# Mixture of experts in sorted blocks of 128 rows, with indirect DMA, in a one-core decoder layer

## The chip, the core and the metric

The kernel runs on one core of a Trainium2 chip. The metric is the device time of one execution in microseconds (us); less is better. Five engines work side by side and meet at semaphores: PE (TensorE, matrix products; its weight loads are listed apart, as PEld), DVE (VectorE), ACT (ScalarE), POOL (GpSimd) and SP (SyncE, which here only issues DMAs). A name with a q (SPq, POOLq) is the sequencer of that engine. A DMA issued by SP or POOL runs on 16 DMA engines that all queues share.

## What is computed

x has 8 batches of 112 tokens of 512 numbers. Three residual steps follow each other: causal self attention, cross attention to a context, and a feed-forward step with experts. Only the last step changes in its algorithm:

```
def _moe(x, gate, expert_bias, w1, w2, w3, shared_w1, shared_w2, shared_w3):
    scores = sigmoid(xt @ gate.T)                        # 896 tokens, 8 experts
    _, sel = top_k(scores + expert_bias, 2)
    top_scores = take_along_axis(scores, sel, axis=1)
    routed = xt[token_idx] * scores_sorted[:, None]      # 1792 rows, one for each choice
    xb = routed.astype(bfloat16)
    for e in range(8):
        h = silu(xb @ w1[e].T) * (xb @ w3[e].T)          # 512 -> 256, bfloat16
        oe = h @ w2[e].T                                 # 256 -> 512
        out_r = out_r + where(expert_ids == e, oe, 0.0)
    hs = silu(xt @ shared_w1.T) * (xt @ shared_w3.T)
    out = hs @ shared_w2.T                               # shared expert, float32
    return out.at[token_idx].add(out_r)
```

The tokens are layer-normalised first, and x is added at the end. Every token has two experts of eight; which ones they are is known only when the gate's scores are there.

## The kernel before

`attention` does both attention steps. Its second part, cross attention, runs 16 steps n (four turns u of four batches s), from about 215 us to 518 us. In each step POOL normalises seven tiles of probabilities (`x_normalise`, L1421) and makes the low parts of the weights that were loaded for the next turn (L1427, L1432). SP loads these weights and contexts in turn order, and waits between them for PE.

`experts` does the last step, in 128-partition tiles of turned tokens (channels on the partitions, tokens in the free dimension), in two halves h of 448 tokens:

- SP loads gate, bias and small tables, writes x to HBM (`x_dram`, L1554) and reads it back in tiles of 128 tokens (`x7`, L1557). POOL loads the experts' matrices with a cast from float32 to bfloat16: w13 of each expert into two buffers (L1569, L1575), w2 of all at once (L1570).
- DVE normalises (`fxn`, L1727). PE turns the eight batches (L1583, into `r_ps`), ACT copies them (`xt`, L1684), DVE makes the high and low parts (L1732, L1716), and PE multiplies all eight batches by the gate (L1590).
- PE runs the shared expert's up projection in four units (`shared_unit`, two for each half; each 24 products of 448 columns, lines 55 to 57). DVE meanwhile takes sigmoid, the two best experts and the weights (L1741 to L1754).
- PE turns the weights (L1650) and spreads an expert's weights over 128 partitions (`spread`, L1610, L1636). DVE scales all tokens by them (`scale_input`, L1771).
- `expert`: for each of 8 experts and both halves, PE does 2 x 16 products of 448 columns (L1624) with a tile of the expert's matrix held in the array and the tokens streamed past it. All 896 tokens go through all 8 experts; a token's weight is zero where it did not choose the expert. ACT takes silu (L1692), DVE multiplies (`hidden`, L1778).
- For seven tiles of 128 tokens, PE adds up 16 products of 512 columns for the experts (L1671) and six of the shared expert in one PSUM bank; DVE adds x (L1807), SP stores (L1561).

PE's program is in order. In `mm3` a float32 product is made of three products of high and low parts:

```
    pe.matmul(out, a_hl[0], b_hl[0], start=start, stop=False, skip_group_check=True)
    pe.matmul(out, a_hl[0], b_hl[1], start=False, stop=False, skip_group_check=True)
    return pe.matmul(out, a_hl[1], b_hl[0], start=False, stop=stop, skip_group_check=True)
```

Of the kernel before, what the change touches and what calls it, by code (L numbers as in the profile page):

```python
# [23 lines left out]
KC = C // 128  # L24
# [13 lines left out]
HC = HID // 128  # L38
EPS = 1e-5
# [48 lines left out]
def build(nc, a, out):  # L88
    with ExitStack() as keep:
# [25 lines left out]

        dve_chain = sem("dve_chain")
        chain_end = [0]

        with ExitStack() as ctx:
            attention(nc, a, sem, sb, ctx, ident, x_sb, xn2_hl, w_raw, p_raw, mask, stats_all, ow_dram, kvn_dram, kvt_dram, aw_dram,  # L120
                      sw_raw, sw_hl, sd_raw, sd_hl, dve_chain, chain_end)
        sb("shared_room", [128, 6 * KC * HID])
        experts(nc, a, sem, sb, ident, x_sb, xn2_hl, sw_hl, sd_hl, stats_all, dve_chain, chain_end, out)


def attention(nc, a, sem, sb, ctx, ident, x_sb, xn2_hl, w_raw, p_raw, mask, stats_all, ow_dram, kvn_dram, kvt_dram, aw_dram,
              sw_raw, sw_hl, sd_raw, sd_hl, dve_chain, chain_end):
# [70 lines left out]
    tile("tail_rest", [128, 936])  # L198
# [59 lines left out]
    qw_loaded, qw_high, qw_low = ([sem(f"qw_{w}{i}") for i in range(4)] for w in ("loaded", "high", "low"))  # L258
    ow_loaded, ow_high, ow_low = ([sem(f"ow_{w}{i}") for i in range(4)] for w in ("loaded", "high", "low"))
# [5 lines left out]
    out_done, x_added = sem("xout_done"), sem("x_added")  # L265
    sw_loaded, sd_loaded, sh_high, sh_low = sem("sw_loaded"), sem("sd_loaded"), sem("sh_high"), sem("sh_low")
# [9 lines left out]
    def ring(n):  # L276
        return FIRST if n == 0 else STARTS if n % HALF == 0 and n < STEPS else LATER

# [25 lines left out]
    with nc.Block() as block:  # L304
        @block.sync
        def _(sp):
# [87 lines left out]
            for u in range(TURNS):  # L394
# [30 lines left out]
        def _(pe):  # L425
# [145 lines left out]
            def query_pair(n, i):  # L571
# [3 lines left out]
                pe.wait_ge(qw_low[i], u + 1)  # L575
# [61 lines left out]
            def x_project(m, i):  # L637
# [4 lines left out]
                pe.wait_ge(ow_low[i], m // HALF + 1)  # L642
# [151 lines left out]
        def _(act):  # L794
# [96 lines left out]
            def x_query_weights_high(u, i):  # L891
                if u < TURNS:
                    act.wait_ge(qw_loaded[i], 32 * u + 32)
                    act.copy(qw[:, i, 0, :], qw_raw[:, i, 1, :]).then_inc(qw_high[i], 1)

            def out_weights_high(u, i):
                act.wait_ge(ow_loaded[i], 16 * u + 16)
                act.copy(ow[i][:, 0], ow_raw[i][:, 1]).then_inc(ow_high[i], 1)  # L898
# [481 lines left out]
        def _(pool):  # L1380
# [43 lines left out]
            def query_weights_low(u, i):  # L1424
                if u < TURNS:
                    pool.wait_ge(qw_high[i], u + 1)
                    pool.tensor_tensor(qw[:, i, 1, :], qw_raw[:, i, 1, :], qw[:, i, 0, :],  # L1427
                                       ALU.subtract).then_inc(qw_low[i], 1)

            def out_weights_low(u, i):  # L1430
                pool.wait_ge(ow_high[i], u + 1)
                pool.tensor_tensor(ow[i][:, 1], ow_raw[i][:, 1], ow[i][:, 0], ALU.subtract).then_inc(ow_low[i], 1)  # L1432

            def shared_low(part):
                pool.wait_ge(sh_high, part + 1)
                raw, high, low = SHARED[part]
                pool.tensor_tensor(low, raw, high, ALU.subtract).then_inc(sh_low, 1)

# [48 lines left out]
def experts(nc, a, sem, sb, ident, x_sb, xn_hl, sw_hl, sd_hl, stats_all, dve_chain, chain_end, out):  # L1487


    HALVES = 2  # L1490
    TILES = N // 128
    x_dram = nc.dram_tensor("x_dram", (N, C), F32).ap()
    rows = out.rearrange("b t c -> (b t) c")
    with ExitStack() as ctx:
# [5 lines left out]
        x7 = tile("x7", [128, TILES, C])  # L1500
        tile("fxn_rest", [128, B * C - TILES * C])
        mean, rstd = tile("mean3", [T, B, 2]), tile("rstd3", [T, B])
        vv, newt = tile("vv3", [T, B]), tile("newt3", [T, B])
        xt = tile("xt", [128, KC, N])
        xt_hl = xn_hl
        gate = tile("gate", [128, KC, EXPERTS])
        bias = tile("bias", [T, EXPERTS])
        iota = tile("iota", [T, EXPERTS])
        pick = tile("pick", [EXPERTS, EXPERTS, 128])
        pick_r = tile("pick_r", [EXPERTS, EXPERTS, 128], F32R)  # L1510
        score = tile("score", [T, B, EXPERTS])
        ranked = tile("ranked", [T, B, EXPERTS])
        best = tile("best", [T, B, 8])
        which = tile("which", [T, B, 8], U32)
        whichf = tile("whichf", [T, B, 2])
        chosen = tile("chosen", [T, 2, B, EXPERTS])
# [360 lines left out]
```

## Time and profile before

| | us |
|---|---|
| median of 3 runs | 661.54 (661.42 to 664.84) |
| the profiled execution | 666.14 |
| its span, from first to last instruction | 664.5 |
| experts stage in it, from 519.3 to 664.5 | 145.2 |

| engine | busy, us | share of the span |
|---|---|---|
| PE | 603.0 | 91% |
| PEld | 460.5 | 69% |
| DVE | 397.4 | 60% |
| ACT | 287.4 | 43% |
| POOL | 246.8 | 37% |

The profile is of one execution. Times of rows are microseconds from the start of the span. The end of a matrix product is modelled, so products that overlap in the pipeline have durations (0.36 us) that are longer than their distance (0.20 us); the chain of work shows the distances. PEclk is the clock granted to PE as a share of full speed.

### The profile page before, as it was taken

Reading aid. Unit: us, or ns where it says so; the run is one execution under the profiler, and the core shown is the slowest. Engines: PE = TensorE matmul, PEld = TensorE weight load, DVE = VectorE, ACT = ScalarE, POOL = GpSimd, SP = SyncE. Lnnn points to the kernel's source line nnn. Section 1 sums busy time; section 2 is a strip of 40 time slices with the busy share of each in tenths; the row PEclk is TensorE's granted clock in tenths of the full one; section 3 lists DMA queues with packets and bytes.
Section 4 is the critical chain, followed back from the end, with each engine's and each line's share of the span. In section 5 each row is a group of like instructions: output and inputs, shape, how many; then the busy total and the mean of one; then the engine's idle time right before and its main releaser. Section 6 shows DMA issues by size and latency. Waiting matters only on the chain. (4 is left out here: it accounts for less than half of the span.)

```text
span 664.5 us, 9657 instructions
## 1 busy us (share of the span) xinstructions
PE 603.0 (91%) x3583; PEld 460.5 (69%) x3586; DVE 397.4 (60%) x844; ACT 287.4 (43%) x629; POOL 246.8 (37%) x225
## 2 busy tenths in 40 slices
PE   2668898998989699999999999999998699999798
PEld 1445676665767488879888888879887498444354
DVE  6654677686675676457664666457663754788411
ACT  3123441633635476447763576447753212322100
POOL 0508732643833355406851387406842100000000
PEclk9968897998979899999999999999999669999899
DMA  8843555665533050013111330005000671343011
GB/s 271 230 151 100 189 178 172 220 193 181 209 127 108 6 152 0 1 50 135 68 47 56 135 111 0 1 14 194 16 1 0 133 227 57 51 76 63 1 48 63
DMA packets 24817, 67.09 MB, mean 101 GB/s; under 512 B 3035, under 2 KB 6573, under 8 KB 24389
## 3 DMA queue, kind: packets, MB, share of 16 engines
q1 hardware_dynamic: 23476, 60.20, 27.4%
q0 software_dynamic: 1296, 6.29, 5.1%
q8 instruction: 29, 0.48, 0.3%
q14 instruction: 16, 0.12, 0.1%
HBM read 56.66 MB, written 16.11 MB: 110 GB/s over the span
## 5 line engine op out<-in xcount | busy, mean ns | idle before, releaser
L1421 POOL TENSOR_TENSOR xprob<-xprob,erec 128x375 f32<-128x375 f32 x112 | 90.2, 812 | 142.6 <-DVE erec L1200 142.4
L888 ACT ACTIVATE xprob<-s_ps,nmax 128x375 f32<-128x375 f32 x112 | 64.2, 574 | 59.8 <-DVE nmax L1195 56.9
L1195 DVE TENSOR_REDUCE nmax<-s_ps 128x1 f32<-128x375 f32 x112 | 59.6, 538 | 0.0
L55 PE MATMUL k_ps<-ow,ctx_hl 128*112 128x512 f32 x128 | 52.5, 410 | 2.8 <-DVE ctx_hl L1190 2.1
L1624 PE MATMUL gu_ps<-xb,w 128*128 128x448 bf16 x256 | 51.2, 353 | 0.4 <-DVE h_all L1778 0.4
L57 PE MATMUL k_ps<-ow,ctx_hl 128*112 128x512 f32 x128 | 50.5, 395 | 0.0
L1190 DVE TENSOR_TENSOR ctx_hl<-k_ps,ctx_hl 128x448 fp32r<-128x448 f32 x32 | 20.0, 624 | 50.6 <-ACT ctx_hl L883 50.6
L56 PE MATMUL k_ps<-ow,ctx_hl 128*112 128x512 f32 x128 | 50.2, 392 | 0.0
L1170 DVE TENSOR_TENSOR pt_hl<-f_ps,pt_hl 125x512 fp32r<-125x512 f32 (+1 forms) x67 | 41.7, 623 | 11.1 <-ACT pt_hl L860 9.8
L55 PE MATMUL s_ps<-kvt,qt_hl 128*128 128x376 f32 x112 | 44.9, 401 | 2.0 <-ACT xprob L888 1.0
L1414 POOL TENSOR_TENSOR prob<-prob,rec 112x1792 f32<-112x1792 f32 x8 | 25.5, 3186 | 54.8 <-DVE rec L1136 54.8
L1692 ACT ACTIVATE act_sb<-gu_ps 128x448 f32<-128x448 f32 x36 | 19.6, 543 | 59.1 <-PE gu_ps L1624 39.8
L860 ACT CAST pt_hl<-f_ps 125x512 fp32r<-125x512 f32 (+1 forms) x67 | 35.6, 533 | 14.1 <-PE f_ps L618 13.8
L1624 PEld LDWEIGHTS gu_ps<-xb,w 128*128 128x128 bf16 x256 | 23.7, 98 | 25.9 <-issue 4.7
L1432 POOL TENSOR_TENSOR ow<-ow_raw,ow 128x1024 fp32r<-128x1024 f32 x16 | 38.3, 2392 | 7.7 <-ACT ow L898 7.7
L618 PEld LDWEIGHTS f_ps<-ident,xprob 128*125 128x125 f32 x236 | 35.4, 189 | 3.8 <-DVE pt_hl L1170 1.0
L56 PE MATMUL s_ps<-kvt,qt_hl 128*128 128x376 f32 x112 | 37.6, 336 | 0.0
L618 PE MATMUL f_ps<-ident,xprob 128*125 128x128 f32 x236 | 37.5, 277 | 0.1
L57 PE MATMUL s_ps<-kvt,qt_hl 128*128 128x376 f32 x112 | 37.6, 335 | 0.0
L55 PE MATMUL k_ps<-pt_hl,kvn 125*128 125x448 f32 x96 | 35.4, 369 | 0.0
L57 PE MATMUL k_ps<-pt_hl,kvn 125*128 125x448 f32 x96 | 35.1, 366 | 0.0
L56 PE MATMUL k_ps<-pt_hl,kvn 125*128 125x448 f32 x96 | 34.9, 364 | 0.0
(208 smaller groups left out, 1495.9 us busy)
## 6 DMA issues: line engine op xcount, KB each, us to landing
ow_raw<-ow_dram SPq DMA_DIRECT2D x16, 512.0 KB, 3.3
raw_b<-in_raw SPq DMA_DIRECT2D x8, 640.0 KB, 5.0
raw_m<-in_raw SPq DMA_DIRECT2D x8, 576.0 KB, 4.8
raw_q<-in_raw SPq DMA_DIRECT2D x8, 512.0 KB, 6.6
ow_dram<-bw_sb SPq DMA_DIRECT2D x8, 512.0 KB, 5.9
qw_raw<-aw_dram SPq DMA_DIRECT2D x16, 256.0 KB, 3.5
w<-in_w POOLq DMA_DIRECT2D x8, 512.0 KB, 5.1
kvt_dram<-kvt_hl SPq DMA_DIRECT2D x8, 376.0 KB
```

Of the source, the lines that this page charges most:

```text
L55: pe.matmul(out, a_hl[0], b_hl[0], start=start, stop=False, skip_group_check=True)
L56: pe.matmul(out, a_hl[0], b_hl[1], start=False, stop=False, skip_group_check=True)
L57: return pe.matmul(out, a_hl[1], b_hl[0], start=False, stop=stop, skip_group_check=True)
L618: mm = pe.transpose(bank[0:LP, j * 128:(j + 1) * 128], xprob[slot(n - 1, k)][:, c * LP:(c + 1) * LP], ident[:, :])
L860: act.copy(dst, src).then_inc(high_copied, 1)
L888: act.activation(xprob[z][:, 0:L], s_bank(n, k)[:, 0:L], ACT.Exp, bias=nmax[:, z:z + 1], accum_out=esum[:, z:z + 1]).then_inc(xexp_done, 1)
L1170: dve.tensor_tensor(dst, src, hi, ALU.subtract).then_inc(emptied, 1)
L1195: dve.tensor_reduce(nmax[:, z:z + 1], s_bank(n, k)[:, 0:L], X, ALU.max, negate=True).then_inc(xmax_done, 1)
L1414: pool.tensor_tensor(prob[q][:, :, :, :], prob[q][:, :, :, :], rec[q][:, :, :].unsqueeze(3).broadcast_to([T, PER, GROUPS, T]), ALU.mult).t ...
L1421: pool.tensor_tensor(xprob[z][:, 0:L], xprob[z][:, 0:L], erec[:, z:z + 1].broadcast_to([128, L]), ALU.mult).then_inc(xp_ready, 1)
L1432: pool.tensor_tensor(ow[i][:, 1], ow_raw[i][:, 1], ow[i][:, 0], ALU.subtract).then_inc(ow_low[i], 1)
L1624: mm = pe.matmul(gu_ps[m][:, w, 0:HT], w13[z][:, w, k, m * 128:(m + 1) * 128], xb[h][:, k, :], start=(k == 0), stop=(k == KC - 1))
```

## The change

In the experts stage the two choices of a token become rows of a table that is sorted by expert, and each expert works only on its own rows, in blocks of 128.

- In cross attention, POOL clears a small tile and numbers the table's spare rows (`lay_blank`, at step 1), and SP fills two tables in HBM (`slots_dram`, one for each half, 14 blocks of 128 rows of 544 bfloat16 each) with zeros and row numbers, behind the loads of turn 0. POOL issues ten DMAs from HBM to HBM, one at the end of each of the steps 2 to 11, that cast w13 and w2 to bfloat16. The semaphores of the weight halves become four common ones instead of 16.
- SP loads all of w13 and w2 (6 MB of bfloat16) at the start of the experts stage. x is not written to HBM and read back any more.
- Turning and gate are done by halves. ACT makes the high part of the turned tokens too.
- `choose`, `count`, `locate`, `owners`: the two best experts of each token; PE counts with a triangular matrix how many tokens before it chose the same expert; DVE works out the row of each choice in the sorted table and the expert that owns each block.
- `lay_rows`: DVE scales the normalised tokens by their weight, in bfloat16, once for each choice. POOL scatters them with 16 indirect DMAs of 112 rows. The order of DVE's program is by halves; `count(1)` of PE stands between the shared units 1 and 2 and waits for `choose(1)`.
- The shared expert's down projection gets a stage of its own: eight batches, x is added in place.
- 28 blocks g. SP loads the block's 128 rows into one of six slots (`xg`); PE turns them (four transposes), ACT copies; PE holds the turned rows and streams the owner's w1 and w3 past them (`up`, four products of 512 columns, the expert's number read into a register by `value_load`); silu on ACT, product on DVE; PE turns the result (two transposes), ACT copies, PE multiplies by w2 (`down`, two products of 512 columns); DVE copies to one of four tiles `o_sb`; POOL scatters the 128 rows with an indirect DMA to HBM (`done_dram`). The list of indices lies in the block's slot.
- SP loads for each token its two rows back (`got`), PE adds them with an identity matrix in one PSUM bank, DVE adds x, SP stores.

The core of the diff:

```diff
+                if u == 0:
+                    sp.wait_ge(blank_ready, 2)
+                    for h in range(HALVES):
+                        rows = slots_dram[h].rearrange("(j p) c -> p j c", p=128)
+                        sp.dma_start(rows[:, :, 0:C], blank[:, :].bitcast(BF16).unsqueeze(1).broadcast_to([128, BLOCKS, C])).then_inc(rows_laid, 16)
+                        sp.dma_start(rows[:, :, C:ROW].bitcast(I32), spare[:, :, :]).then_inc(rows_laid, 16)
...
+                if n == 1:
+                    lay_blank()
+                if 2 <= n < 2 + EXPERTS:
+                    pool.dma_start(w13_dram[n - 2], a["w13"][n - 2]).then_inc(w_cast, 16)
+                if 2 + EXPERTS <= n < 4 + EXPERTS:
+                    z = n - 2 - EXPERTS
+                    es = slice(z * EXPERTS // 2, (z + 1) * EXPERTS // 2)
+                    pool.dma_start(w2_dram[:, es], a["w2"][:, es]).then_inc(w_cast, 16)
...
+    RING, SENT = 6, 4
+    EARLY = BLOCKS + RING + 1
...
+                def load_slots(g):
+                    h, j, z = g // BLOCKS, g % BLOCKS, g % RING
+                    if j == 0:
+                        sp.wait_ge(sent[h], 16 * TOP2 * HALF)
+                    if g >= RING:
+                        sp.wait_ge(xg_turned, g - RING + 1)
+                        sp.wait_ge(put[(g - RING) % SENT], 16 * put_by(g - RING + 1)[(g - RING) % SENT])
+                    sp.dma_start(xg[z][:, :], slots_dram[h][j * 128:(j + 1) * 128]).then_inc(xg_loaded[z], 16)
...
+                for g in range(ALL):
+                    pool.wait_ge(o_copied, g + 1)
+                    to = xg[g % RING][:, C:C + 2].bitcast(U32)
+                    pool.indirect_dma_start(done_dram[g // BLOCKS], bass.IndirectOffsetOnAxis(ap=to, axis=0),
+                                            o_sb[g % SENT][:, :], None).then_inc(put[g % SENT], 16)
...
+                def up(g):
...
+                    e = pe.value_load(own_e[0:1, h, j:j + 1], min_val=0, max_val=EXPERTS - 1)
+                    pe.wait_ge(xg_copied, g + 1)
+                    wait(pe, hid_done, g - 1)
+                    for k in range(KC):
+                        mm = pe.matmul(b_ps[g % 2][:, :], xgt[g % 2][:, k, :], w13[:, e, :, k, :], start=(k == 0), stop=(k == KC - 1))
...
+                shared_unit(0)
+                count(0)
                 shared_unit(1)
...
+                count(1)
                 shared_unit(2)
...
                 shared_unit(3)
...
+                for b in range(B):
+                    shared_down(b)
+                pe.wait_ge(tri_ready, 3)
+                pe.wait_ge(d_added, B)
+                turn_slots(0)
+                turn_slots(1)
+                pe.wait_ge(w_loaded, 16 * 6)
+                owner = [up(0)]
+                for g in range(ALL):
+                    if g + 2 < ALL:
+                        turn_slots(g + 2)
+                    if g + 1 < ALL:
+                        owner.append(up(g + 1))
+                    turn_hidden(g)
+                    if g:
+                        down(g - 1, owner[g - 1])
+                    if EARLY <= g < EARLY + HALF:
+                        gather(g - EARLY)
+                down(ALL - 1, owner[ALL - 1])
+                for b in range(HALF, B):
+                    gather(b)
...
+                shared_hidden(0)
+                locate(0)
+                for b in range(HALF):
+                    lay_rows(b)
+                choose(1)
+                owners(0)
+                shared_hidden(1)
+                shared_hidden_low(0)
+                locate(1)
...
+                for g in range(ALL):
+                    hidden(g)
+                    if g >= 2:
+                        copy_out(g - 2)
+                    if EARLY < g <= EARLY + HALF:
+                        result(g - EARLY - 1)
```

## Rows read from the trace of the kernel before

**Rows 1.** Busy time by stretch: us (instructions) per engine, PEclk, DMA share, GB/s
```profile
246.00:290.00 44.00, 44.00 (x244) 38.43 (x243) 24.97 (x57) 24.19 (x59) 19.23 (x19) 1.00 0.00 1
...
320.00:420.00 100.00, 99.97 (x555) 87.83 (x554) 62.29 (x149) 62.13 (x151) 55.67 (x54) 1.00 0.19 66
...
519.00:540.00 21.00, 15.94 (x98) 14.79 (x99) 14.55 (x49) 4.52 (x10) 1.78 (x3) 0.60 0.88 191
...
565.00:625.00 60.00, 56.41 (x273) 26.61 (x271) 47.69 (x50) 17.56 (x33) 3.16 (x6) 1.00 0.31 53
625.00:664.50 39.50, 35.62 (x151) 18.75 (x154) 4.96 (x8) 0.00 (x0) 0.00 (x0) 0.94 0.13 47
```

**Rows 2.** Chain that ended last, experts stage: start, us on it, engine, tile, line, count
```profile
524.06 6.47 PE r_ps L1583 x32
530.53 9.06 PE w_ps L1590 x64
539.59 0.57 PE gu_ps L55
...
551.26 0.77 PE w_ps L1650 x8
...
556.85 1.00 PE r_ps L1610 x4
...
566.65 3.19 PE gu_ps L1624 x16
...
625.51 5.09 PE gu_ps L1671 x15
...
651.48 3.47 PE gu_ps L1671 x16
656.35 3.47 PE gu_ps L1671 x16
```

**Rows 3.** Instructions grouped by line, from 508 to 665 us: busy us, mean ns
```profile
L1692 ACT ACTIVATE act_sb<-gu_ps 128x448 f32<-128x448 f32 x36 | 19.6, 543 | 59.1 <-PE gu_ps L1624 39.8 <-PE gu_ps L57 19.3
...
L1807 DVE TENSOR_TENSOR y_sb<-x,gu_ps 128x512 f32<-128x512 f32 x7 | 4.8, 687 | 32.1 <-PE gu_ps L57 32.1
L1684 ACT COPY xt<-r_ps 128x448 f32<-128x448 f32 x8 | 4.2, 533 | 13.0 <-PE r_ps L1583 13.0
L1727 DVE TENSOR_SCALAR fxn<-x_sb,mean,rstd 112x512 f32<-112x512 f32 x8 | 3.7, 538 | 0.0
```

**Rows 4.** Timeline: start, us, engine, line; transposes, and DVE from scores to weights
```profile
500.16 1.04 PE L618 MATMUL f_ps<-ident,xprob 128*125 128x128 f32 x8
...
539.88 0.20 DVE L1741 TENSOR_SCALAR score<-score 112x64 f32<-112x64 f32 x1 [5.39 <-ACT score L1686]
...
545.77 0.23 DVE L1754 TENSOR_TENSOR chosen<-chosen,score 112x64 f32<-112x64 f32 x1
...
547.07 0.63 DVE L1759 TENSOR_TENSOR hs<-gu_ps,act_sb 128x448 f32<-128x448 f32 x1 [1.07 <-ACT act_sb L1692]
```

**Rows 5.** Busy time by stretch, around PE's idle time ahead of L1671
```profile
622.00:625.50 3.50, 0.00 (x0) 0.13 (x2) 2.76 (x5) 0.36 (x1) 0.00 (x0) 1.00 0.00 0
625.50:629.10 3.60, 3.59 (x9) 1.31 (x9) 0.00 (x0) 0.00 (x0) 0.00 (x0) 0.53 0.02 5
```

**Rows 6.** DMA issues: count, KB each, median us to landing; last, POOL's issuing instruction in ns
```profile
w<-in_w POOLq DMA_DIRECT2D x8, 512.0 KB, 5.1
...
out<-y_sb SPq DMA_DIRECT2D x7, 256.0 KB, 2.0
...
qw_raw<-in_kr SPq DMA_DIRECT2D x16, 64.0 KB, 3.3
...
L1575 POOL DMA_DIRECT2D w<-in_w x6: 527/527/527, 570.5 to 607.8; - x6
```

**Rows 7.** Timeline of POOL in cross attention, end of one step and start of the next
```profile
260.14 1.55 POOL L1427 TENSOR_TENSOR qw<-qw_raw,qw 128x640 fp32r<-128x640 f32 x1
263.60 0.81 POOL L1421 TENSOR_TENSOR xprob<-xprob,erec 128x375 f32<-128x375 f32 x1 [1.91 <-DVE erec L1200]
```

More of the change, by code:

```diff
@@ L38 @@
 HC = HID // 128
+HALVES, TOP2 = 2, 2
+BLOCKS = TOP2 * HT // 128 + EXPERTS - 1
+ROW = C + 32
+SPARE = TOP2 * HT
 EPS = 1e-5
@@ L1509, in experts @@
[L1509 to L1516, printed above, removed]
-        wt_hl = tile("wt_hl", [EXPERTS, 2, N], F32R)
-        w13 = [tile(f"w13_{z}", [128, 2, KC, HID], BF16) for z in range(2)]
+        with ExitStack() as laid:
+            xt = sb("xt", [128, KC, N], F32, laid)
@@ L1547, in experts, with put_by @@
+        def put_by(g):
+            return [sum(1 for k in range(g) if k % SENT == z) for z in range(SENT)]
         with nc.Block() as block:
@@ new lines, in turn_hidden, with down @@
+                def turn_hidden(g):
+                    pe.wait_ge(hid_done, g + 1)
+                    wait(pe, hid_copied, g)
+                    bank = h_ps[:, :].bitcast(BF16)
+                    for m in range(HC):
+                        mm = pe.transpose(bank[:, m * 128:(m + 1) * 128], hid[g % 2][:, m * 128:(m + 1) * 128], ident_bf[:, :])
+                    mm.then_inc(hid_turned, 1)
+                def down(g, e):
+                    pe.wait_ge(hid_copied, g + 1)
+                    wait(pe, o_copied, g - 1)
+                    for m in range(HC):
+                        mm = pe.matmul(o_ps[g % 2][:, :], hid_t[g % 2][:, m, :], w2[:, e, m, :], start=(m == 0), stop=(m == HC - 1))
+                    mm.then_inc(o_done, 1)
@@ new lines, in gather @@
+                def gather(b):
+                    pe.wait_ge(got_loaded[b // HALF], 16 * HALF)
+                    wait(pe, y_ready, b)
+                    for r in range(TOP2):
+                        mm = pe.matmul(c_ps[0:T, :], ident_bf[0:T, 0:T], got[:, b, r, :], start=(r == 0), stop=(r == TOP2 - 1))
+                    mm.then_inc(c_done, 1)
+                for b in range(HALF):
+                    turn_tokens(b)
+                pe.wait_ge(small_loaded, 64)
+                route(0)
@@ new lines, in _ @@
+                for b in range(B):
+                    shared_down(b)
[15 more added lines that the diff above has]
+                        gather(g - EARLY)
@@ new lines, in lay_rows, with shared_hidden @@
+                def lay_rows(b):
+                    h, s = b // HALF, b % HALF
+                    for r in range(TOP2):
+                        dve.tensor_scalar(rows[:, b, r, 0:C], xn[:, b, :], weight[:, h, r, s:s + 1], None,
+                                          ALU.mult).then_inc(rows_ready, 1)
+                def shared_hidden(u):
+                    half, m = u // HC, u % HC
+                    dve.wait_ge(silu_done, u + 1)
+                    dve.tensor_tensor(hs[:, m, half * HT:(half + 1) * HT], gu_ps[u % 2][1][:, 0:HT], act_sb[u % 2][:, :],
+                                      ALU.mult).then_inc(h_done, 1)
@@ new lines, in hidden, with copy_out @@
+                def hidden(g):
+                    dve.wait_ge(up_silu, g + 1)
+                    wait(dve, hid_turned, g - 1)
+                    dve.tensor_tensor(hid[g % 2][:, :], b_ps[g % 2][:, HID:2 * HID], up_sb[g % 2][:, :], ALU.mult).then_inc(hid_done, 1)
+                def copy_out(g):
+                    z = g % SENT
+                    dve.wait_ge(o_done, g + 1)
+                    if g >= SENT:
+                        dve.wait_ge(put[z], 16 * put_by(g)[z])
+                    dve.tensor_copy(o_sb[z][:, :], o_ps[g % 2][:, :]).then_inc(o_copied, 1)
@@ new lines, in _ @@
+                for b in range(HALF):
+                    tile_low(b)
+                choose(0)
+                for b in range(HALF, B):
+                    tile_low(b)
+                shared_hidden(0)
+                locate(0)
+                for b in range(HALF):
+                    lay_rows(b)
[4 more added lines that the diff above has]
+                locate(1)
+                for b in range(HALF, B):
+                    lay_rows(b)
@@ L1811 @@
+                copy_out(ALL - 1)
+                for b in range(HALF, B):
+                    result(b)
 def kernel(**inputs):
```

532 lines of the change are left out of this document (304 added, 228 removed).

## The prediction

> **What bounds the kernel now.** I read the busy time by stretch first. Through cross attention PE has work for 99.97 of 100 us at full clock, while POOL has 56 [rows 1]: PE is the bound there, and what the change adds on POOL and SP costs only what reaches PE. In the experts stage PE is busy 56.4 of the 60 us of the experts' up projection and 35.6 of the last 39.5 us, with the DMA engines at 31% and 13% [rows 1]. The chain of work that ended last says the same: it runs over PE's products one behind the other [rows 2]. So the stage of 145.2 us (519.3 to 664.5) is bound by PE's columns, and fewer columns would help. The first 21 us are another matter: clock 0.60, DMA engines at 88% [rows 1]. DMA latency is nowhere on the chain; every transfer of this stage is loaded early or stored late. The question for the change is whether it stays so.
>
> **Part 1, cross attention.** POOL gets ten DMA issues. One took 0.53 us, for 128 rows [rows 6]; they stand where POOL sat idle for 1.91 us between two steps [rows 7], so I cost them at nothing. Without that cover it would be 10 x 0.53 = 5 us. POOL's two small instructions at step 1 go with them. The transfers themselves use engines that are 19% busy [rows 1]. SP's four fills (3.7 MB) wait for POOL's step 1 and start near 254 us. Behind them on SP stand only the loads of turn 1, from 289 us, and the DMA engines moved nothing from 246 to 290 us [rows 1], so 35 us of cover. The removed semaphores only merge counts that rise in the same order. I take 0 for the whole part, and -1 to +5 as bounds.
>
> **Part 2, up to the shared expert.** Turning takes 6.47 us for 8 batches and the gate 9.06 us [rows 2]; by halves they are the same instructions on PE in another order. ACT now copies each batch twice, 2 x 0.53 us [rows 3], against 0.81 us of turning, but the gate products between the halves let it catch up. So the first shared unit begins at 539.6, as before [rows 2]. The write of x to HBM goes away; nothing waited for it. From 539.59 to 551.26 there are two units, and one unit at full clock takes 556.85 - 552.03 = 4.82 us [rows 2]; the first, half of it at the lower clock, takes 6.85. The counting is some eight small products like L1650, 0.8 us [rows 2]. PE: unit 0 to 546.5, count(0) to 547.3, unit 1 to 552.1.
>
> Now count(1) waits for choose(1), and DVE is late. Its program: shared_hidden(0) ends at about 547.9 (before it was 547.07 + 0.63 [rows 4]); locate(0) has 9 small instructions of 0.2 us (as L1741 [rows 4]), 1.9 us; eight lay_rows at 3.7 us for eight (L1727 [rows 3]); choose(1): scores to weights took 539.88 to 546.00 for eight batches [rows 4], for four some 4.0. That is 557.5, so PE idles 5.4 us, with units 2 and 3 queued behind the wait. What this does to the clock is in the trace: PE was idle for 3.5 us (622.0 to 625.5) and then ran 3.6 us at 0.53 [rows 5], its 15 products taking 5.09 us where 16 take 3.47 later [rows 2]. That is 1.8 us more; I take 2.0. So count(1) to 558.4, unit 2 to 565.2, unit 3 to 570.0. The shared down projection: two tiles of the last stage are 656.35 - 651.48 = 4.87 us apart, less the experts' 3.47 [rows 2] is 1.40 us for six products; times 8 batches is 11.2, to 581.2. It was inside the last stage before, 7 x 1.40 = 9.8. The loop then waits for the last addition (0.69, L1807 [rows 3], and 0.2): 582.1. The rows of both halves are scattered and loaded by then (DVE's last rows are laid near 567, eight indirect DMAs behind). 6 MB of weights go at the 191 GB/s of the first stretch [rows 1] in 33 us, to about 555: covered.
>
> **Part 3, PE's work in a block.** Four products of 512 columns for up and two for down, at 3.47/16 = 0.217 us [rows 2]: 1.30 us. Six transposes of 128 rows: eight took 1.04 us with the pipeline's end, some 0.12 apart [rows 4], and I take 0.1: 0.6. Together 1.9; with bubbles 2.0 us. 28 blocks are 56 us, against the 60 + 7 x 3.47 = 84 us for the experts before. ACT has three instructions a block, 0.58 + 0.37 + 0.37 scaled from 0.53 and 0.54 us for 448 columns [rows 3], 1.3 us; DVE 0.4 + 0.6 = 1.0. Neither binds. value_load stands ahead of each up; the trace has nothing like it. Bounds: 0 (PE's queue covers it) and a round trip as long as the shortest DMA, 2.0 [rows 6]; I take 0, since the sequencer reaches it with the last down and the next transposes, 0.8 us, still to run, and since the next part leaves room for it. The Trainium skill (DMA: Bandwidth & Descriptors, Latency and other measured facts) gives such a load a floor of 0.6 us; by that it would be covered too. No row here shows it.
>
> **Part 4, the slots' ring.** This is what I expect to decide. Slot g is loaded only when block g-6's scatter has landed, because its index list lies in that slot. down(g-6) is the last work of PE's round g-5, and turn_slots(g) the first of round g-2: PE has two rounds between, 4 us. On the other side lies a chain of memory round trips:
> - down's end to o_sb copied: 0.2 pipeline end, 0.15 behind hidden(g-4), 0.6 for 512 columns (L1807 took 0.69 with two inputs [rows 3]): 0.95;
> - the indirect scatter of 128 KB, not in the trace. Lower bound 2.0, the store of 256 KB by SP; upper bound 5.1, POOL's casting load of 512 KB [rows 6]. It is a small store, near the lower row, plus POOL's work for 128 indices, for which I put twice POOL's 0.53 us issue [rows 6]: 3.1;
> - SP's load of 136 KB: between 2.0 and 3.3 [rows 6], taken as 2.2;
> - semaphores: 0.2.
>
> Sum 6.45 us for two rounds, so 3.2 us a block and not 2.0. With the bounds: 5.0 and, with 5.1 and 3.3, 9.6; I hold 8.2 for likely enough. The ring acts on rounds 4 to 25: 11 pairs. Up(0) ends at 582.1 + 0.4 + 0.7 + 0.9 = 584.1; three rounds to 590.1; 11 x 6.45 = 71.0, to 661.1; three more rounds to 666.6. The four-deep ring of o_sb asks 0.6 + 3.1 + 0.1 every four blocks and is slack.
>
> The page named above (Anatomy of one DMA — SWDGE (gpsimd) path) puts a DMA of POOL at about 2.0 us plus its bytes, 2.3 us for the scatter. By that the ring turns in 5.65 and the sum below ends near 671. It would give 4.4 us for the 1 MB source of w, and the row has 5.1 [rows 6].
>
> **Part 5, the tail.** After the last round: down 0.65, copy 0.65, scatter 3.1, three more issues of SP of 0.45 each, load 2.2, then a chain in one PSUM bank: 4 x (two products 0.65 + addition 0.69 + 0.05) = 5.5, store 2.0, end 0.5: 16.0. Before, only a store lay behind PE.
>
> **Sum.** 666.6 + 16.0 = 682.6 against a span of 664.5: +18.1. The profiled execution took 666.14 and the runs' median is 661.54, so the span is 3 us over the median; I add the difference to the median: 679.6.
>
> **Rivals.**
> - *The ring is slack* (faster than before). If scatter and load together take under 4.0 - 1.15 = 2.85 us, PE's 2.0 us is the pace: 584.1 + 56 + 16 = 656.1, -8.4, so 653.1. For it: the DMA engines are idle. Against it: already two of the shortest transfers of the trace are 4.0 [rows 6].
> - *PE falls to the lower clock in the loop.* At 1.2 GHz a block is 1.85 x 2 = 3.7 us: 584.1 + 103.6 + 16 = 703.7, so 700.8. For it: the ring gives PE gaps of 2.5 us every two rounds, and 3.5 us of idling lowered the clock [rows 5]. Against it: the gaps are shorter, and at 3.7 us a block there is no gap left. A slow value_load of 2 us gives the same number. The Trainium skill (TensorE: Matmul & The Clock Gate, HAM oscillation) tells of kernels in which each round starts cold behind a DMA wait; by it this rival holds, and the trace agrees as far as its one long gap goes.
> - *Cross attention suffers*: casts or fills delay PE. With part 1's upper bound 684.6, and more where casts are slow.
> - *The blocks save no columns.* Not so: 28 x 128 rows are padded, but their count is fixed, 3584 rows for 7168.
>
> **How the numbers follow.** Forecast (ring binds) 0.62, with its own range 662 (5.0 us, shorter tail) to 701 (8.2 us); ring slack 0.12; lower clock or slow register load 0.18; cross attention 0.08. A measurement of this kernel can tell some 0.5% (3.3 us) from no change. Faster: the slack ring and 0.04 of the forecast's low end, 0.16. Same: 0.08 from the low end, where the round trips are near 5.0, and 0.01 of the rest, 0.09. Slower 0.75. The range goes from 655, just above the slack ring, to 704, just above the lower clock.
>
> **What would show it.** In the profile after: idle time of PE ahead of the slots' transposes, released by the DMA of xg, in every second round, and turn_slots 6.4 us apart for two rounds; POOL's indirect DMAs with some 3 us to landing; a gap of 5 us ahead of count(1), with a lower clock behind it; the last down some 16 us ahead of the end; PE still 99.97 of 100 us busy in cross attention. I am wrong if an indirect DMA and a load together land within 3 us, if PE's rounds are even, if value_load holds PE longer than the ring does, or if the waits inside the loop end at POOL, because an indirect DMA keeps it for more than 3.2 us.

## The result, and the profile after

| | before | after |
|---|---|---|
| median, us | 663.19 (661.42 to 665.28, 4 runs) | 694.21 (692.97 to 699.51, 4 runs) |
| ratio, 95% interval | | 1.0482 [1.0413, 1.0551] |
| profiled execution, span | 666.14, 664.5 | 693.14, 691.3 |

The change makes the kernel 4.8% slower. Predicted were 679.6 us with a range of 655 to 704: the side is right, the size is 14.6 us short of the measured time. The span and the busy time of the page after:

```profile
span 691.3 us, 10138 instructions
PE 584.0 (84%) x3552; PEld 455.8 (66%) x3552; DVE 391.8 (57%) x908; ACT 307.0 (44%) x688; POOL 294.2 (43%) x290
```

Busy time by stretch: in cross attention, from the start of the experts stage to its first block, in the loop, behind it, and the whole stage (columns as in [rows 1]):

```profile
320.00:420.00 100.00, 99.97 (x545) 87.20 (x545) 61.29 (x148) 60.51 (x149) 57.40 (x59) 1.00 0.37 96
...
515.00:587.00 72.00, 55.78 (x256) 49.28 (x256) 38.48 (x144) 12.95 (x27) 18.61 (x34) 0.74 0.36 128
589.00:669.00 80.00, 56.60 (x330) 28.38 (x327) 29.26 (x57) 32.70 (x81) 23.73 (x25) 0.91 0.34 102
670.00:691.00 21.00, 5.16 (x12) 1.23 (x10) 4.07 (x6) 0.14 (x1) 2.92 (x3) 0.59 0.37 112
...
514.00:691.00 177.00, 119.11 (x608) 79.94 (x608) 73.64 (x209) 47.29 (x111) 45.87 (x62) 0.81 0.34 111
```

The same view of before, from 519 to 664 us:

```profile
519.00:664.00 145.00, 132.96 (x639) 81.57 (x642) 79.82 (x145) 27.79 (x52) 4.94 (x9) 0.91 0.34 82
```

The blocks do save PE work: 119.1 us of it in this stage where there were 133.0. But the stage is 177 us long and no longer 145: PE idles 58 us in it, where it idled 12. Those are the lines to explain. Who PE waited for, by stretch: first from the stage's start to the first block, then in the loop. Columns: us in total, times, longest.

```profile
PE e_ps L59 <- DVE x_sb L1960: 7.9, 1, 7.9
PE e_ps L1686 <- DVE fxn L1988: 6.3, 1, 6.3
PE e_ps L1705 <- DVE both L1910: 3.8, 1, 3.8
```

```profile
PE e_ps L1744 <- DMA xg<-slots_dram: 17.7, 9, 2.7
PE e_ps L1755 <- issue: 3.7, 9, 0.6
PE e_ps L1755 <- ACT xgt L1843: 1.9, 3, 0.7
```

The 6.3 us at L1686 are not new: before waits 6.2 us for the same products. New are the 7.9 us at L59 (called the hole below), the 3.8 us at L1705 and the waits of L1744 and L1755 in the loop. L1744 turns a slot, and it waits nine times for the load of xg. One turn of the ring, in the chain that ended last (start, us, what):

```profile
593.45 0.69 DVE o_sb L1972
594.15 0.27 issue
594.41 2.42 DMA done_dram<-o_sb,xg
...
596.89 2.47 DMA xg<-slots_dram
599.37 0.05 issue
599.41 0.41 PE e_ps L1744 x4
```

That is the chain that the prediction drew: copy, scatter 2.42, load 2.47, some 6.2 us from the end of down. Yet the timeline of PE shows the wait in every third round, not in every second:

```profile
599.41 0.40 PE L1744 MATMUL e_ps<-fident_bf,xg 128*128 128x128 bf16 x4 [2.66 <-DMA xg<-slots_dram]
...
601.93 0.39 PE L1744 MATMUL e_ps<-fident_bf,xg 128*128 128x128 bf16 x4
...
603.94 0.39 PE L1744 MATMUL e_ps<-fident_bf,xg 128*128 128x128 bf16 x4
604.54 1.03 PE L1755 MATMUL e_ps<-w,xgt 128*128 x4 [0.21 <-issue]
...
608.47 0.40 PE L1744 MATMUL e_ps<-fident_bf,xg 128*128 128x128 bf16 x4 [2.35 <-DMA xg<-slots_dram]
609.32 1.89 PE L1755 MATMUL e_ps<-w,xgt 128*128 x4 [0.46 <-issue]
```

Three rounds take 9.06 us here. The round behind a wait may run at the lower clock: the four products of L1755 took 1.89 us at 609.32 and 1.03 at 604.54.

### The profile page after: what moved, and what is told of

Read it like the earlier page. It is cut to its first block and busy times, and to the rows that moved or that the text cites. A ratio compares the mean times of both kernels' runs of the same rounds, so it can differ in the third digit from the quotient of the medians.

```text
span 691.3 us, 10138 instructions
## 1 busy us (share of the span) xinstructions
PE 584.0 (84%) x3552; PEld 455.8 (66%) x3552; DVE 391.8 (57%) x908; ACT 307.0 (44%) x688; POOL 294.2 (43%) x290
## 5 line engine op out<-in xcount | busy, mean ns | idle before, releaser
L1677 POOL DMA_INDIRECT done_dram<-o_sb,xg x28 | 27.2, 971 | 77.5 <-DVE o_sb L1972 76.9
L59 PE MATMUL k_ps<-ow,ctx_hl 128*112 128x512 f32 x128 | 52.5, 410 | 2.5 <-DVE ctx_hl L1215 1.9
L60 PE MATMUL k_ps<-ow,ctx_hl 128*112 128x512 f32 x128 | 50.2, 392 | 0.0
L1195 DVE TENSOR_TENSOR pt_hl<-f_ps,pt_hl 125x512 fp32r<-125x512 f32 (+1 forms) x67 | 41.7, 623 | 11.2 <-ACT pt_hl L885 10.1
L59 PE MATMUL s_ps<-kvt,qt_hl 128*128 128x376 f32 x112 | 45.1, 403 | 2.0 <-ACT xprob L913 1.0
L1965 DVE TENSOR_TENSOR hid<-e_ps,up_sb 128x256 bf16<-128x256 f32 x28 | 11.9, 425 | 51.4 <-ACT up_sb L1849 49.6
L60 PE MATMUL s_ps<-kvt,qt_hl 128*128 128x376 f32 x112 | 37.8, 337 | 0.0
L1755 PE MATMUL e_ps<-w,xgt 128*128 x112 | 32.5, 417 | 6.2 <-issue 3.7
L61 PE MATMUL s_ps<-kvt,qt_hl 128*128 128x376 f32 x112 | 37.7, 337 | 0.0
L59 PE MATMUL k_ps<-pt_hl,kvn 125*128 125x448 f32 x96 | 35.4, 368 | 0.0
```

Of the source, the lines that this page charges most:

```text
L1195: dve.tensor_tensor(dst, src, hi, ALU.subtract).then_inc(emptied, 1)
L1677: pool.indirect_dma_start(done_dram[g // BLOCKS], bass.IndirectOffsetOnAxis(ap=to, axis=0), o_sb[g % SENT][:, :], None).then_inc(put[g % S ...
L1755: mm = pe.matmul(b_ps[g % 2][:, :], xgt[g % 2][:, k, :], w13[:, e, :, k, :], start=(k == 0), stop=(k == KC - 1))
```

## The experiments

Each states its ratio to the kernel before, with 95% interval, where it was timed against it. S(i) is the start of the slots' transposes (L1744) in round i, which turn slot i+2. "First block" is the start of the very first of them, counted from the first statistics of the experts stage (514.96 us in the changed kernel, 519.83 in before).

### Ring of eight slots, and of five

```diff
-    RING, SENT = 6, 4
+    RING, SENT = 8, 4
-    EARLY = BLOCKS + RING + 1
+    EARLY = BLOCKS + 7
```

The other kernel has 5 in the place of 8. The kernel with eight slots also merges two semaphores with others, which the lines above leave out.

> Ring of gathered slots of 8 instead of 6 (two semaphores merged with others of the same engine to make room; nothing else is moved). In the trace of the changed kernel a round of the loop starts 6.4 us after the round that last used its slot has gone out: copy 0.7, scatter 2.4, load 2.4 and the issues. Its work lies in the round itself, so the recurrence there is over three rounds: 3 rounds in work 2.0-2.5 + 6.5 = 9.1-9.9 us. Theory A (slot ring): with 8 slots it is over five rounds, 8.5/5 = 1.7 us, below TensorE's own 1.9 us; the idle between rounds goes, rounds 3 to 25 take 22 x 1.9 = 42 us where they took 70.8, and the whole 664 to 670 us. Rival B (rate of the indirect DMAs or of the memory): the pace stays 3.0-3.2 us a block however many slots there are, 690-696 us. Rival C (clock): TensorE drops to the half clock at the loop's duty and a round costs 2.9 us, 685-694 us.

> Ring of 5 slots instead of 6, nothing else changed. Two readings of the ring give different doses. As the prediction put it (a slot's 6.45 us chain over R-4 rounds: two rounds with six slots): 6.45 us for every round, rounds 3 to 25 take 142 us, whole 765 us. As the trace of the changed kernel shows (work of one round 2.0-2.5 us plus 6.5 us over R-3 rounds): 4.3-4.5 us a round, 95-99 us, whole 718-723 us. If the ring does not set the pace: 694 us.

Eight slots: 665.21 us, ratio 1.0015 [0.9983, 1.0047]; S(3) to S(25) takes 48.9 us (588.61 to 637.48) instead of 70.8 (594.80 to 665.59). Five slots: 730.45 us, one run; S(3) to S(25) takes 106.6 us (594.52 to 701.10), 4.8 a round. Eight slots came out in the expected range. Five came out above the 718 to 723 us that were expected from the second reading, though far from the 765 of the first. PE's waits in the loop with five slots, and the timeline of PE with eight:

```profile
PE e_ps L1744 <- DMA xg<-slots_dram: 39.2, 12, 5.0
```

```profile
602.25 0.39 PE L1744 MATMUL e_ps<-fident_bf,xg 128*128 128x128 bf16 x4
602.69 1.03 PE L1755 MATMUL e_ps<-w,xgt 128*128 x4
603.57 0.28 PE L1764 MATMUL e_ps<-fident_bf,hid 128*128 128x128 bf16 x2
603.68 0.60 PE L1771 MATMUL e_ps<-w,hid_t 128*128 x2
604.11 0.39 PE L1744 MATMUL e_ps<-fident_bf,xg 128*128 128x128 bf16 x4
```

1.86 us a round, no wait. So the ring decides, and neither the rate of the DMAs (rival B) nor the clock (rival C) does: both fall, since the same transfers now go at 1.9 us a block. The dose settles how the ring counts. The chain, some 6.5 us with the signals, starts at the *end* of round i-3, and round i-3 has its own 2.0 to 2.5 us of work behind its start: from wait to wait S(i) = S(i-3) + 8.6 to 9.9 with six slots (up to S(19)), and mostly S(i) = S(i-2) + 9.4 with five. The prediction's own form (6.45 us for every round with five slots) asked for 142 us and 765. The second reading asked for 95 to 99 us where 106.6 were measured; it had taken 2.0 to 2.5 us for the work of a round, and with five slots both rounds of a turn ran at the lower clock (the four products of L1755 took 1.89 and 1.91 us at 614.23 and 617.40, against 1.03 above). The 48.9 us, against 42 expected, hold one thing more, ahead of slot 22 in round 20:

```profile
625.68 0.61 PE L1744 MATMUL e_ps<-fident_bf,xg 128*128 128x128 bf16 x4 [3.30 <-DMA xg<-slots_dram]
626.53 1.89 PE L1755 MATMUL e_ps<-w,xgt 128*128 x4 [0.25 <-issue]
```

SyncE had issued the four loads of got (L1636, 0.9 MB) at 617.91 to 619.91, and the load of this slot behind them at 620.02. So the wait is put down to them. In the kernel with four edits below, where these loads are spread over four slot loads, the wait at this place is gone.

### Rows of the second half scattered late

```diff
                 for g in range(ALL):
...
+                    if g < TOP2 * HALF:
+                        send_rows(1, g // TOP2, g % TOP2)
```

with the eight scatters of the second half taken out ahead of the loop.

> The eight scatters of the second half of the tokens are issued one behind each of the loop's first eight scatters and no longer while the shared part runs (which needs them only at round 14). Theory S (the storm of scattered rows holds up TensorE's signals): the hole of 7.9 us in the shared part ahead of the third sum, where ScalarE's activation of the last shared unit starts at 571.1 although its matmuls were streamed by 564.6, goes, and with it the half clock behind it (3 us); the loop begins 10 us earlier and the whole takes 684 us. Against it stands that GpSimd then spends 2.5 us a block in the first eight rounds (under the 3.2 of the ring; 0 to 4 us more). Rival T (the hole has nothing to do with the scatters, say a fetch of instructions at that place): hole stays at the same instruction, 694 to 698 us.

689.41 us, ratio 1.0403 [1.0358, 1.0448], where 684 was expected. The hole is not there and the first block starts 63.2 us behind the stage's start (72.5 in the changed kernel). This alone says nothing about the scatters, since the kernels with eight and with five slots, which ran on the same chip, keep the scatters and show no hole either; the run that can tell stands below. From the first block to the last product of a block it takes 85.4 us. The changed kernel takes 83.0, 85.0 and 85.1 in its three traces, so no loss in the loop is shown. POOL does hold two DMAs a block, 1.25 to 1.28 us each, and a ring scatter queues behind a row scatter:

```profile
588.67 0.94 POOL L1670 DMA_INDIRECT slots_dram<-rows,slot_u  x1 [0.30 <-issue]
589.92 0.97 POOL L1680 DMA_INDIRECT done_dram<-o_sb,xg  x1 [0.31 <-issue]
```

### VectorE chooses for the second half first

```diff
-                for b in range(HALF):
-                    lay_rows(b)
                 choose(1)
+                for b in range(HALF):
+                    lay_rows(b)
```

> VectorE picks the second half's experts before it writes the first half's 8 rows tiles (3.25 us) instead of behind them; nothing else changed. Theory: TensorE's idle of 3.75 us ahead of the second count falls to 0.5 or nothing, and the 3.4 us at half clock behind it goes (1.5 us): up to 4-5 us earlier, 689-690 us; the first half's scatters begin 3 us later, and that must not show, since the loop begins 30 us behind them. Rival: if the hole of 7.9 us further on is tied to the scatters (which now end no earlier), it grows by what is gained here: 694 us.

685.14 us, ratio 1.0311 [1.0248, 1.0375]. The wait ahead of the second count is down from 3.8 us to 0.5, as expected:

```profile
PE e_ps L59 <- DVE hs_hl L1956: 2.0, 1, 2.0
PE e_ps L1744 <- issue: 0.8, 1, 0.8
PE e_ps L1705 <- DVE both L1910: 0.5, 1, 0.5
```

Its first block starts at 61.5 us. Against the 65.1 of both ring kernels, which have the old order, that is 3.6 us for the order. The time is under the 689 to 690 us expected, because the hole is not in this trace either.

First blocks have to be compared with an eye on the clock. The late-rows kernel began its first block at 63.2 us here and at 65.3 in its second trace (below), with the same waits (3.7 and 1.4 us): the granted clock from the first shared unit to the first block was 0.92 and then 0.86. Over the four shared units it was 0.88 in the first trace of the changed kernel as in the first late-rows trace, and 0.78 in the kernel with eight slots as in the second late-rows trace. So of the 11 us between 61.5 and 72.5, 3.6 are the order and 9.4 (72.5 - 63.2) the hole with the lower clock behind it, less some 2 that the clock of the shared units gave back.

### The hole: the changed kernel again, and again

> The changed kernel itself, not a letter changed. In its first trace TensorE streamed the last shared unit's matmuls by 564.6 us, but the signal behind them is recorded at 571.08, together with those of the two sums behind it (571.15, 571.23), and in that hole of 7.9 us lies half of what the prediction missed ahead of the loop. None of the four kernels with one edit each shows the hole. Theory F (belongs to this program, whatever the cause): the same hole at the same signal, loop begins at 587 to 588, 693 to 695 us. Rival G (an event of one execution): no hole, the loop begins at 579 to 582, the profiled run takes 684 to 688, and the median of the runs lies between 684 and 694.

> The changed kernel once more, not a letter changed. Both traces of it show the hole: signals of TensorE that arrive 5 to 6.5 us behind the end of their matmuls, together, while the second half's rows are scattered and the first slots are loaded; with it the updates of VectorE and ScalarE of these 10 us are missing from the trace. The traces of the four kernels with one edit each show none, but they ran together on another chip than the second trace of the changed kernel, so program and chip can't be told apart yet. Theory F (the program's): hole again, first block of the loop at 72 us after the start of the experts' stage, 692 to 700 us. Rival K (the chip's, or the occasion's): no hole, first block at 65 us, 684 to 689 us.

696.18 and 696.81 us, first block at 72.1 and 72.2 us, and the hole in both. ScalarE's activations of the last two shared units (L1833), in the first trace of the changed kernel, in its second, and in the kernel with eight slots:

```profile
561.10 0.55 ACT L1833 ACTIVATE act_sb<-e_ps 128x448 f32<-128x448 f32 x1 [11.08 <-PE e_ps L61]
571.10 0.54 ACT L1833 ACTIVATE act_sb<-e_ps 128x448 f32<-128x448 f32 x1 [9.01 <-remote]
```

```profile
567.41 0.55 ACT L1833 ACTIVATE act_sb<-e_ps 128x448 f32<-128x448 f32 x1 [12.46 <-remote]
576.04 0.54 ACT L1833 ACTIVATE act_sb<-e_ps 128x448 f32<-128x448 f32 x1 [7.63 <-remote]
```

```profile
562.98 0.54 ACT L1833 ACTIVATE act_sb<-e_ps 128x448 f32<-128x448 f32 x1 [10.90 <-PE e_ps L61]
567.78 0.55 ACT L1833 ACTIVATE act_sb<-e_ps 128x448 f32<-128x448 f32 x1 [3.80 <-PE e_ps L61]
```

The two units are 4.8 us of PE apart, as in the last fence. They come 10.0 and 8.6 us apart where the hole is. "Remote" says that the signal came so long after the product that it can't be paired with it: PE streamed the unit's last product at 564.24 and its signal is recorded at 571.08. So rival G falls and F holds for this program: it is no event of one execution. In the two later traces PE's wait is 6.9 us, and the first block comes 7 us behind the 65.1 to 65.3 of the traces with the same clock and no hole.

> The kernel whose second-half scatters are issued behind the loop's first eight scatters, unchanged, on the same chip as the changed kernel's third run. If the changed kernel shows the hole here and this one doesn't, the scatters and the slot loads at the same time are its cause (first block 63 us after the start of the stage, 688-691 us); if both show it, the traffic is not; if neither does, it is the chip's or the occasion's, and this run adds nothing.

689.66 us (two runs), ratio 1.0391 [1.0344, 1.0438]; on the same chip as the third run of the changed kernel (696.81 us, first block at 72.2), with the scatters late, there is no late signal of PE ahead of the loop. First block at 65.3 us. This is the pair that points to the scatters of the second half, with one trace of each.

> The kernel with only VectorE's order changed, unchanged, in a further run. The four kernels of the first call (eight slots, five slots, late scatters, this order) ran on one chip and their traces show no late signal; every trace with scatters taken elsewhere shows late signals or missing updates at 38 to 46 us behind the start of the stage. Theory K (the chip's): on another chip this kernel shows them too, its first block begins 65 to 69 us behind the start of the stage instead of 61.5, and its time is 687 to 693 us instead of 685.1 median. Rival L (the order of VectorE removes them): 61.5 us, 683 to 687 us.

687.09 us, ratio 1.0381 [1.0327, 1.0434]; first block at 64.5 us, 3.0 more than on the first chip at nearly the same clock, and 2.4 us of it are waits of PE for the shared sums; VectorE starts one addition some 3.2 us behind the end of its products. So theory K holds for the late signals, though the first block came just under the 65 us that it asked for. The medians, 685.14 and 687.09, are 2 us apart, and their intervals overlap. What stands: outside the first four experiments, late signals ahead of the loop are in every trace in which the second half's scatters run beside the shared part (seven), and in neither of the others (late scatters; no scatters). Three of the first four kernels, which ran on one chip, have those scatters there too and show none. Why the occasion matters is open, and chip and occasion are not told apart. The same traces lack updates of VectorE and ScalarE in these microseconds, so the recording itself may have a part in the delay, and no run here separates the two. The second late-rows trace lacks such updates as well and has no late signal, so a gap in the record doesn't by itself bring the delay.

### The first part alone

> The first part (self and cross attention) of the changed kernel with the experts' part of the kernel before: the casts of the experts' weights to bf16 in DRAM, the fills of the block lists, the blank tiles and the counted semaphores run, and nothing uses what they write; the experts are computed as before. The prediction put the first part at 0 (bound +2). Theory: 661 to 664 us and an experts' stage that starts at 515 to 520, since TensorE is busy 99.9% of the cross attention with and without the casts. Rival H (the new first part is itself faster by the 2.3 to 4.9 us by which the five traces of it are ahead of the one of before at the start of the experts' stage): 657 to 660 us. Rival I (the casts disturb what follows, their writes being in flight when the weights are loaded again): 666 us or more.

663.84 us, ratio 0.9998 [0.9972, 1.0024]. Cross attention with the casts, and before in [rows 1]:

```profile
320.00:420.00 100.00, 99.97 (x553) 87.74 (x552) 61.97 (x148) 62.40 (x152) 58.97 (x59) 1.00 0.40 103
```

The stage starts at 520.4 us, and in the three traces of the changed kernel at 515.0, 519.2 and 519.3. The 4.9 us by which its first trace was ahead of before are there already at POOL's first tile of cross attention (209.97 against 214.92 us) and are the spread of the first 200 us between executions. Rivals H and I fall.

### Four edits together

Ring of eight, VectorE's order, the loads of got one behind each of four slot loads, and

```diff
+        def sum_ps(b):
+            return c_ps if b < HALF else t_ps[b % 2]
...
-                        mm = pe.matmul(c_ps[0:T, :], ident_bf[0:T, 0:T], got[:, b, r, :], start=(r == 0), stop=(r == TOP2 - 1))
+                        mm = pe.matmul(sum_ps(b)[0:T, :], ident_bf[0:T, 0:T], got[:, b, r, :], start=(r == 0), stop=(r == TOP2 - 1))
```

with four tiles of y_sb instead of two.

> Four edits together: ring of eight slots; VectorE picks the second half's experts ahead of the first half's rows; the four loads of the first half's results are issued one behind each of four slot loads instead of in a row (in the trace with eight slots TensorE waits 3.3 us at round 22 for a slot queued behind them, and runs that round at half clock, 1.0 us more); the last four sums alternate between two PSUM banks with four result tiles, so that TensorE no longer waits 0.9 us for each addition. Expected from 665.2 us with the ring alone: -3.5 (count), -4 to -5 (loads), -3 (sums): 652 to 657 us. If the ring of eight only hides a pace that the DMA queues set, the loads spread over four rounds cost stalls of 1 us in each, and it stays at 660. Nothing of the computation is left out.

> The kernel with four edits, unchanged, beside the one above on the same chip. 658 to 661 us as before where the signals are late (first block 65 us after the start of the stage), 655 to 657 where they are not.

> The kernel with four edits, and SyncE holds the first slot loads until five of the eight shared sums are added, so that they no longer run beside the scatters of the second half. In the trace with four edits TensorE's signals came up to 2.9 us late there and its first block began 65.4 us after the start of the stage, against 61.5 in the kernel with only VectorE's order changed. If loads beside scatters hold up the signals: no late signal, first block at 61.5 to 62, 3.5 us faster than the same kernel without the wait. If it's the scatters alone: still late, no difference. The wait itself: loads land 2.5 us after the fifth sum, 2 us before the first block needs them, so it costs nothing.

660.12 us, ratio 0.9945 [0.9926, 0.9964]; again, 658.00, 0.9920 [0.9890, 0.9951]; with the slot loads held, 655.87, 0.9890 [0.9858, 0.9922]. All three intervals lie below 1, so these kernels are 0.5 to 1.1% faster than the kernel before. The first of them was expected at 652 to 657 us. By the traces, the loop and the tail gave what was expected over the kernel with eight slots: S(3) to S(25) takes 44.9 us instead of 48.9, and from there to the end 23.3 instead of 26.0. The 3.5 us of VectorE's order did not come: the first block stands at 65.4 us as before, with late signals ahead of it. The 660 us of a pace set by the DMA queues would have come with a stall in each of four rounds, and the trace has only one wait for a slot, of 0.2 us.

With the loads held, the first block comes at 62.5 us instead of 65.3. That doesn't show that the loads had a part in the hole. From the first shared unit to the first block (held, then not), PE idles 6.2 us with the loads held and 5.4 without; the clock makes the difference, 0.96 against 0.86:

```profile
537.20:577.60 40.40, 34.17 (x161) 28.03 (x162) 23.90 (x79) 5.70 (x10) 16.55 (x16) 0.96 0.25 75
```

```profile
536.90:580.00 43.10, 37.71 (x161) 30.51 (x161) 24.09 (x79) 5.70 (x10) 16.54 (x16) 0.86 0.23 72
```

The signals were late all the same: VectorE starts additions up to 2.4 us behind the end of their products. Whether holding the loads brings the higher clock, and with it the 2.1 us of the median, one trace of each can't tell. The loop with four edits, at full clock, and what stands behind it:

```profile
582.00:637.00 55.00, 50.45 (x329) 27.11 (x326) 29.36 (x58) 33.23 (x82) 24.21 (x25) 1.00 0.46 138
637.00:655.00 18.00, 4.47 (x11) 1.42 (x10) 4.40 (x7) 0.01 (x1) 2.91 (x3) 0.70 0.47 145
...
514.00:655.00 141.00, 112.20 (x608) 78.05 (x608) 72.74 (x208) 47.41 (x111) 46.01 (x62) 0.84 0.43 140
```

PE still idles 29 of the stage's 141 us. The four sums behind the loop now take 3.77 us, against 6.93 in the changed kernel (680.90 to 687.83):

```profile
647.71 3.77 PE L1787 MATMUL e_ps<-got,fident_bf 112*112 112x512 bf16 x8 [9.96 <-DMA got<-done_dram]
```

## Why the prediction was right and where it was wrong

The profiled span came out at 691.3 where 682.6 was summed, +8.7 us: -4.9 for a stage that began earlier, +10.3 to the first block, -1.8 in the loop, +5.1 behind it.

**Part 1 (0): right.** Ratio 0.9998 for it alone.

**Part 2 (first block 62.3 us behind the stage's start of before; it is 72.5): +10.3, the step that failed.** The stall at count(1) was named rightly and sized 5.4 us; it is 3.8. The unit behind it ran partly at 0.5 of the clock, as [rows 5] had it. The gate's products were taken over from [rows 2] at 9.06 us; at a clock of 0.50 they take 2 x 6.0:

```profile
531.00:537.10 6.10, 6.10 (x36) 6.10 (x34) 2.78 (x7) 1.76 (x5) 0.00 (x0) 0.50 0.43 175
```

In before the clock was 0.66 there (530.5 to 539.6). But this did not reach the first block: count(1) begins 37.8 us behind the stage's start where 37.7 was predicted, since the gate's excess and the estimates for the first unit and VectorE that were too long cancel, by luck, and the first shared sum begins at 49.5 where 50.2 was predicted. The whole miss lies in the eight shared sums behind it. They were put at 8 x 1.40 = 11.2 us with no wait. The third waits for the addition of the first, and that stands in VectorE's program behind the hidden values of the last unit: 1.4 us in the kernels with five and eight slots, which have no hole. In the changed kernel the hole makes this wait 7.9 us, and the 15 products behind it run at a clock of 0.50, 0.43 us apart instead of 0.23, 3.0 us more. Together 10.9 us. The wait of 1.4 could be read from the program's order. The hole could not be read from the trace of before: it has no indirect DMA. The prediction had named no cost for scatters beside PE, only for their landing, and should have bounded it. What causes the hole stays open, as said above.

**Part 3 (2.0 us a block): right.** 1.86 to 1.9 us with eight slots. value_load was taken at 0, with 0 to 2.0 as bounds. It takes 0.30 us on PE's sequencer and lies under the products:

```profile
L1751 PEldq TENSOR_LOAD <-own_e x28: 296/302/522, 587.6 to 666.6; - x28
```

The floor of 0.6 us that the Trainium skill (DMA: Bandwidth & Descriptors, Latency and other measured facts) gives is twice what this load from SBUF took.

**Part 4 (71.0 us for rounds 3 to 25; 70.8): right in the mechanism, and in the sum by two errors that cancel, which is luck.** The two later traces of the changed kernel have 72.9. The chain was 6.45 us by the sum and measured 6.37 from S(2) to S(4), with the scatter at 2.42 (3.1 taken) and the load at 2.47 (2.2 taken). But it was laid over two rounds, as if S(i-2) were the end of round i-3. It is so only where round i-2 has not waited itself. Over three rounds with 2.0 us of work, 8.45 us, the loop would have been 62 us. The other 9 us are the products behind a wait at half clock (0.9 us a turn), a scatter that queues on POOL behind the one before, and the slot queued behind got (3.3 us of waiting with eight slots). Five slots tell the two readings apart, six do not. Two slips in the working are small: three rounds from 661.1 end at 667.1, not 666.6, and with a scatter of 2.3 us the sum ends near 673, not 671. The clock of the second rival is in the trace, but as a fraction: 0.91 over the loop, and 1.00 once the waits are gone. The page TensorE: Matmul & The Clock Gate of the Trainium skill (HAM oscillation) tells of kernels whose rounds start at the lower clock behind a DMA wait. The trace agrees for some of the rounds behind a wait with six slots, and for both rounds of the turn shown with five.

**Part 5 (16.0 us; 21.1 from the last down, 670.2): +5.1.** The terms were right in kind. Missed: three scatters stand in a row on POOL, 1.27 us apart, since the last three blocks finish within 3 us; the four loads landed 4 us after their issue, not 2.2; and PE, 10.0 us idle, ran the sums at half clock.

```profile
670.26 0.97 POOL L1677 DMA_INDIRECT done_dram<-o_sb,xg  x1 [0.70 <-DVE o_sb L1972]
671.53 0.97 POOL L1677 DMA_INDIRECT done_dram<-o_sb,xg  x1 [0.30 <-issue]
672.81 0.97 POOL L1677 DMA_INDIRECT done_dram<-o_sb,xg  x1 [0.31 <-issue]
...
680.90 1.10 PE L1778 MATMUL e_ps<-got,fident_bf 112*112 112x512 bf16 x2 [10.02 <-DMA got<-done_dram]
682.87 1.07 PE L1778 MATMUL e_ps<-got,fident_bf 112*112 112x512 bf16 x2 [0.87 <-DVE y_sb L1978]
```

The rest of the 14.6 us is no step: the span of before's profiled execution (664.5) stood 3.0 us over the median then known, and that of after (691.3) stands 2.9 under its own, 694.21.

## What to carry to other kernels

A ring that is refilled through memory has a period: its chain plus the work of the round that the chain starts from, divided by the rounds between; write it as a recurrence of starts and see for which depth it falls under the engine's own pace. Here 8.5/3 is over 1.9 us and 8.5/5 under it, and two more slots were worth 22 us of the loop, more than the 14 us of PE work that the blocks saved. A saving of PE work is only worth what PE is not made to wait for: from the last product of a block to the end, copy, scatter, load, sum and store take some 20 us, where before ends 3.3 us behind its last product (661.2 to 664.5), so count that price before the columns. And compare the start of a stage between two traces only together with the granted clock ahead of it: here the clock alone moved it by 2 us.

## What the runs showed of the hardware

- An indirect scatter of 128 rows of 1 KB from SBUF to DRAM takes 0.97 us of GpSimd, 1.27 us from one to the next, and 2.4 us from issue to landing in the loop.
- A register load from SBUF on TensorE's sequencer takes 0.30 us (median of 28; the longest took 0.52).
- While indirect scatters run back to back, ScalarE and VectorE can start 2.4 to 6.5 us behind the end of the products that they wait for, though these are streamed on time; some 7 us of the result hang on it (696.81 against 689.66 us on one chip), and its cause is not settled.
- The same program starts its experts stage anywhere from 515 to 519 us (three traces): the first 200 us vary by 4 us between executions.
